# An adapter's up product folded into the next weights, one root for double norms, attention dots in column parts, and a narrow matrix in three parts

## What is computed

```python
# L0 graph attention, second layer (one head): two dots per node, then a softmax over its edges
alpha_s = einsum('nhc,hc->nh', h, a_s); alpha_d = einsum('nhc,hc->nh', h, a_d)
# L2 graph block: adapter, then two graph convolutions (A: the 128 x 128 normalised adjacency)
h = relu(x @ Wd + bd) @ Wu + bu + x        # 768 -> 24 -> 768, with residual
h = relu(A @ (h @ W1) + b1)                # 768 -> 256
h = A @ (h @ W2) + b2                      # 256 -> 768
# L2 ffn: two quantised products of rms-normed rows, 768 -> 2*32 and 32 -> 768
# L3 graph block: relu(A1 @ (xn @ W1) + b1), then A1 @ (. @ W2) + b2, both 768 x 768
# L3 ffn: a router and an attention, each on a layernorm of the block's layernormed rows; MLP 768 -> 48 -> 768
```

## Time and profile before

| | before |
|---|---|
| median of 3 runs | 376.37 us |
| the profiled execution: time, span | 376.2 us, 374.4 us |
| PE busy | 360.3 us, 96% of the span |
| PE in the chain that ended last (VectorE) | 91% (7%) of the span |
| VectorE, ScalarE, GpSimd busy | 180.8, 65.9, 42.1 us |
| granted TensorE clock, mean | 0.986 |
| read from HBM | 89.45 MB, 240 GB/s over the span |

### The profile page before, as it was taken

The page is one execution under the profiler, slowest core; times in us unless marked ns, Lnnn a source line. Parts: engine busy times, 40 slices in busy tenths (PEclk is TensorE's granted clock), DMA queues, the critical chain, the costliest instruction groups (busy, mean ns, idle before and its releaser), DMA issues.

```text
span 374.4 us, 4198 instructions
## 1 busy us (share of the span) xinstructions
PE 360.3 (96%) x1596; PEld 228.4 (61%) x1596; DVE 180.8 (48%) x542; ACT 65.9 (18%) x152; POOL 42.1 (11%) x70
## 2 busy tenths in 40 slices
PE   7999999899999999898899999989999999999997
PEld 3566665556565765555456555464565599966654
DVE  4936525584847465467626635426622301163341
ACT  2012110101111200112002311023123311064010
POOL 4900000020000002040040000302030200000000
PEclk9999999999999999998999999999969999999999
DMA  7999999987955253099999999746251600000001
GB/s 281 412 403 425 437 414 417 370 342 277 348 207 217 105 207 134 15 428 412 412 419 380 420 430 372 289 188 246 63 213 27 268 2 0 2 0 3 0 0 42
DMA packets 10453, 90.10 MB, mean 241 GB/s; under 512 B 2146, under 2 KB 2786, under 8 KB 6338
## 3 DMA queue, kind: packets, MB, share of 16 engines
q1 hardware_dynamic: 8238, 84.91, 56.7%
q0 software_dynamic: 800, 3.54, 2.5%
q10 hardware_dynamic: 1396, 1.40, 1.1%
HBM read 89.45 MB, written 0.39 MB: 240 GB/s over the span
## 4 chain that ended last, share of the span: by engine, by line
PE 91%; DVE 7%; issue 1%; POOL 0%; ACT 0%; POOLq 0%; DVEq 0%
PE ps L1486 14%; PE ps L1452 13%; PE ps L1837 8%; PE ps L1431 6%; PE ps L1664 4%; PE ps L1645 4%; PE ps L1474 3%; PE ps L1751 2%; PE ps L1363 2%; PE ps L1515 2%; PE ps L1817 2%; PE ps L1913 2%; PE ps L1703 2%; PE ps L1885 2%; PE ps L1933 2%; PE ps L1553 2%
## 5 line engine op out<-in xcount | busy, mean ns | idle before, releaser
L1452 PE MATMUL ps<-ring,xT 128*128 128x512 f32 (+1 forms) x168 | 56.4, 486 | 0.0
L1486 PE MATMUL ps<-ring,h 128*128 128x512 f32 (+1 forms) x168 | 55.6, 486 | 0.0
L1486 PEld LDWEIGHTS ps<-ring,h 128*128 128x128 f32 x168 | 31.2, 190 | 21.9 <-issue 20.1
L1452 PEld LDWEIGHTS ps<-ring,xT 128*128 128x128 f32 x168 | 30.8, 191 | 19.5 <-issue 17.7
L792 DVE CUSTOM_DVE_ANT_0 g<-h,avec 128x768 f32<-128x768 f32 x9 | 8.6, 959 | 36.3 <-ACT h L500 24.8
L375 POOL TENSOR_TENSOR rstd<-var,mhalf 128x1 f32<-128x1 f32 x10 | 6.5, 646 | 170.4 <-DVE var L734 83.2
L1431 PE MATMUL ps<-ring,xT 128*128 128x512 f32 (+1 forms) x72 | 24.2, 490 | 0.1
L500 ACT ACTIVATE h<-ps 128x768 f32<-128x768 f32 (+6 forms) x22 | 13.3, 614 | 61.6 <-PE ps L1452 16.2
L880 DVE TENSOR_SCALAR ring<-ring,idxb,ewb 128x128 bf16<-128x128 bf16 x99 | 22.5, 311 | 0.0
L1431 PEld LDWEIGHTS ps<-ring,xT 128*128 128x128 f32 x72 | 13.6, 193 | 9.3 <-issue 8.5
L500 ACT ACTIVATE xT<-ps 128x256 f32<-128x256 f32 (+2 forms) x20 | 7.9, 394 | 56.9 <-PE ps L1379 30.1
(11 more groups left out here) (383 smaller groups left out, 520.4 us busy)
## 6 DMA issues: line engine op xcount, KB each, us to landing
ring<-in_gat_w SPq DMA_DIRECT2D x15, 2304.0 KB, 11.1
avec<-in_gat_a SPq DMA_DIRECT2D x9, 768.0 KB, 8.9
ring<-in_l_w SPq DMA_DIRECT2D x3, 2304.0 KB, 34.3
ring<-in_gat_w SPq DMA_DIRECT2D x6, 384.0 KB, 6.3
ring<-in_l_w SPq DMA_DIRECT2D x2, 1152.0 KB, 6.3
ring<-in_l1f_w1a SPq DMA_DIRECT2D x1, 2304.0 KB, 21.2
ring<-in_l1f_w1b SPq DMA_DIRECT2D x1, 2304.0 KB, 25.8
ring<-in_l1f_w2a SPq DMA_DIRECT2D x1, 2304.0 KB, 30.8
```

The lines of the kernel that those rows point to most:

```text
L1452: last = mm(ps[:, at + lo:at + hi], xT[:, c, :], w[:, c, lo:hi], start=(c == 0), stop=(c == C - 1))
L1486: last = mm(ps[:, 4 * WIN + lo:4 * WIN + hi], h2[:, par * D + c * P:par * D + (c + 1) * P], w[:, c, lo:hi], start=False, stop=False)
```

## The change

- The up product and `l2_w1` are multiplied with each other first (25 x 256), from the weights alone: six small transposes of `l2_wu`, a ScalarE copy, six matmuls, a ScalarE copy to `up_first`. They stand where fillers stood in the first block's ffn end. In the L2 graph block `xT @ l2_w1` starts on the rows themselves, one 25-row matmul adds the adapter, and the adjacency is applied to 256 columns instead of 768.
- The second norm's root is one power of the first variance: 1/sqrt(v(1+e2) + e1 e2). In the L3 ffn both roots come from one two-column instruction, and `xn` is computed later.
- Head 8's dots are taken in two parts: 512 columns from `h1`, 256 columns from PSUM; then a two-element sum. Fifteen edges instead of eight stand behind `score_row`.
- `middle_weights` has three parts of 256 columns; the third stands behind the ffn, between the two halves of L1782, and the L3 stage works in column halves around it. The fold rows of the MLP's norm are made two at a time (2-column outputs) and stand behind the adjacency.
- FIRST_SLOT is 0: units 0 to 3 go into the slots of the head weights as these come free; unit 4 is the first to wait for `edges_summed`.

The core of the diff (index shifts of semaphore counts left out):

```diff
@@ units, names
-FIRST_SLOT = 4
+FIRST_SLOT = 0
-        mhalf = sb("mhalf", [P, 1])
+        mhalf2 = sb("mhalf2", [P, 2])
+        mhalf = mhalf2[:, 0:1]
         released = [("l0_weights_used", 1), ("rows_ps", 6), ("hid1_mm", 2), ("hid1_mm", 4), ("w2a_used", 1),
-                    ("rows_ps", 8), ("rows_ps", 10), ("early_ps", 4), ("rows_ps", 14)]
+                    ("rows_ps", 8), ("rows_ps", 10), ("early_ps", 6), ("rows_ps", 14)]
+        twice, both_var, both_root = cell("twice"), cell("both_var", 2), cell("both_root", 2)
+        wuT, up_first = attnT[:].rearrange("p a b -> p (a b)")[:, 0:C * (DOWN + 1)], att[0:DOWN + 1].rearrange("p a b -> p (a b)")
@@ sync
             load_avec(7)
             load_w2(6, 0)
+            sp.wait_ge(S["hprod"], 7)
+            load_unit(0)
             load_w2(7, 1)
             load_avec(8)
-            sp.wait_ge(s("edges_summed"), 1)
-            for u in range(len(UNITS)):
+            for u in range(1, len(UNITS)):
+                if u == 1:
+                    sp.wait_ge(S["hprod"], 8)
+                if u == 2:
+                    sp.wait_ge(S["w2_used"], 7)
+                if u == 3:
+                    sp.wait_ge(S["hprod"], 9)
                 if u == 4:
-                    sp.wait_ge(S["hprod"], 7)
...
+                    sp.wait_ge(s("edges_summed"), 1)
@@ gpsimd
-            def inverse_root_twice(k, eps):
-                inverse_root(k)
-                pool.wait_ge(s("rstd_ready"), roots[0])
-                link(pool.tensor_tensor(again[:, 0:1], rstd[:], rstd[:], ALU.mult))
-                link(pool.tensor_tensor(again[:, 0:1], again[:, 0:1], mv[:, 1:2], ALU.mult))
-                link(pool.tensor_scalar(again[:, 0:1], again[:, 0:1], eps, None, ALU.add))
-                link(pool.tensor_tensor(again[:, 0:1], again[:, 0:1], mhalf[:], ALU.pow))
-                pool.tensor_tensor(twice, again[:, 0:1], rstd[:], ALU.mult).then_inc(s("rstd_ready"), 1)
...
+            def inverse_root(k, root=rstd[:], of=var[:], half=mhalf):
+                pool.wait_ge(s("var_ready"), k)
+                pool.tensor_tensor(root, of, half, ALU.pow).then_inc(s("rstd_ready"), 1)
...
-            inverse_root_twice(6, RMS_EPS)
+            inverse_root(6, twice)
...
-            inverse_root_twice(9, LN_EPS)
+            inverse_root(10, both_root, both_var, mhalf2[:])
@@ scalar
+            act.wait_ge(s("l2_ps"), 1)
+            copy(wuT, bank(6, C * (DOWN + 1))).then_inc(s("l2_copied"), 1)
+            act.wait_ge(s("l2_ps"), 2)
+            copy(up_first, bank(1, HID2, 0, DOWN + 1)).then_inc(s("l2_copied"), 1)
             part_T(3)
...
             def middle_weights(n):
-                act.wait_ge(s("early_ps"), 2 + n)
-                copy(wo_mid[:, n * D // 2:(n + 1) * D // 2], bank(3 - n, D // 2, 0, BIT)).then_inc(s("early_copied"), 1)
+                act.wait_ge(s("early_ps"), (2, 3, 6)[n])
+                copy(wo_mid[:, n * 256:(n + 1) * 256], bank((3, 2, 7)[n], 256, 0, BIT)).then_inc(s("early_copied"), 1)
...
-            for n, (lo, hi) in enumerate(HALVES):
-                act.wait_ge(s("early_ps"), 5 + n)
-                copy(g1[:, lo:hi], ps[:, 2 * WIN + lo:2 * WIN + hi]).then_inc(s("early_copied"), 1)
+            act.wait_ge(s("early_ps"), 5)
+            copy(g1[:, 0:WIN], bank(2)).then_inc(s("early_copied"), 1)
+            middle_weights(2)
+            act.wait_ge(s("early_ps"), 7)
+            copy(g1[:, WIN:D], bank(3, D - WIN)).then_inc(s("early_copied"), 1)
+            act.wait_ge(s("early_ps"), 9)
+            nc.scalar.activation(xn[:, WIN:D], bank(3, D - WIN), ACT.Relu).then_inc(s("early_copied"), 1)
             act.wait_ge(s("mlp_ps"), 1)
-            copy(fold_row, bank(7, 2 * MLP, 0, 1)).then_inc(s("mlp_copied"), 1)
+            copy(fold_row, bank(7, MLP, 0, 2)).then_inc(s("mlp_copied"), 1)
+            part_T(7)
             act.wait_ge(s("mlp_ps"), 2)
             copy(fold_rows, bank(7, 2 * MLP, 2 * P)).then_inc(s("mlp_copied"), 1)
@@ vector
+            share = cell("alpha_share", 4)
+            dve.wait_ge(s("gat2_rows"), 1)
...
+            for k in range(2):
+                link(nc.vector.tensor_tensor_reduce(g3[:, 0:WIN], h1[:, 0:WIN], avec[:, k * D:k * D + WIN], 1.0, 0.0, ALU.mult,
+                                                    ALU.add, share[:, k:k + 1]))
             dve.wait_ge(S["hprod"], 9)
+            for k in range(2):
+                link(nc.vector.tensor_tensor_reduce(g3[:, WIN:D], bank(5, D - WIN), avec[:, k * D + WIN:(k + 1) * D], 1.0, 0.0,
+                                                    ALU.mult, ALU.add, share[:, 2 + k:3 + k]))
+            nc.vector.tensor_tensor(alpha[:, 0, :], share[:, 0:2], share[:, 2:4], ALU.add).then_inc(S["alpha_ready"], 1)
             nc.vector.tensor_copy(h1[:, WIN:D], bank(5, D - WIN)).then_inc(S["h_rows"], 1)
-            dve.wait_ge(s("gat2_rows"), 1)
-            head_alphas(8, 0)
+            wait(dve, "alpha_ready", 9)
             head_softmax(8, 0)
...
-            for n, (lo, hi) in enumerate(HALVES):
-                dve.wait_ge(s("l2_ps"), n + 2)
-                nc.vector.tensor_tensor(g1[:, lo:hi], ps[:, lo:hi], xn[:, lo:hi], ALU.add).then_inc(s("node_rows"), 1)
-            part_T(6)
             dve.wait_ge(s("l2_ps"), 4)
-            nc.vector.tensor_scalar(g2[:, 0:HID2], bank(7, HID2), 0.0, None, ALU.max).then_inc(s("node_rows"), 1)
+            nc.vector.tensor_copy(g2[:, 0:HID2], bank(0, HID2)).then_inc(s("node_rows"), 1)
+            dve.wait_ge(s("l2_ps"), 5)
+            nc.vector.tensor_scalar(g1[:, 0:HID2], bank(1, HID2), 0.0, None, ALU.max).then_inc(s("node_rows"), 1)
...
-            nc.vector.tensor_scalar(var[:], mv[:, 1:2], LN_EPS, None, ALU.add).then_inc(s("var_ready"), 1)
+            nc.vector.tensor_scalar(var[:], mv[:, 1:2], 1.0 + RMS_EPS, RMS_EPS * LN_EPS, ALU.mult, ALU.add) \
+                .then_inc(s("var_ready"), 1)
...
-            whiten(10)
-            nc.vector.tensor_scalar(xn[:], x[:], mv[:, 0:1], rstd[:], ALU.subtract, ALU.mult).then_inc(S["dve_step"], 1)
...
+            nc.vector.tensor_scalar(both_var[:, 1:2], mv[:, 1:2], 1.0 + LN_EPS, LN_EPS * LN_EPS, ALU.mult, ALU.add) \
+                .then_inc(s("var_ready"), 1)
+            nc.vector.tensor_scalar(both_var[:, 0:1], mv[:, 1:2], LN_EPS, None, ALU.add).then_inc(s("var_ready"), 1)
...
             affine_T("zhatT_ps", g1, "ln1", "xaT_ready")
+            link(nc.vector.tensor_scalar(xn[:], x[:], mv[:, 0:1], both_root[:, 0:1], ALU.subtract, ALU.mult))
@@ tensor
-            sum_edges(range(10, 25))
+            sum_edges(range(10, 18))
             score_row(8, 0)
-            sum_edges(range(25, EC)).then_inc(s("edges_summed"), 1)
+            sum_edges(range(18, EC)).then_inc(s("edges_summed"), 1)
...
-            stay_warm(1, 0)
+            wait_unit(pe, U_L2)
+            w = unit(U_L2, "l2_wu")
+            for c in range(C):
+                last = tr(bank(6, DOWN + 1, c * (DOWN + 1)), w[:, c * P:(c + 1) * P], ident[0:DOWN + 1, 0:DOWN + 1])
+            last.then_inc(s("l2_ps"), 1)
...
             pe.wait_ge(s("adj_ready"), 2)
-            warm_until(7, "var_ready", 3)
-            warm_until(4, "rstd_ready", 3)
+            w = unit(U_L2, "l2_w1", "p (c n) -> p c n", c=C)
+            pe.wait_ge(s("l2_copied"), 1)
+            for c in range(C):
+                last = mm(bank(1, HID2, 0, DOWN + 1), wuT[:, c * (DOWN + 1):(c + 1) * (DOWN + 1)], w[:, c, :], start=(c == 0),
+                          stop=(c == C - 1))
+            last.then_inc(s("l2_ps"), 1)
+            warm_until(1, "rstd_ready", 3)
             stay_warm(2)
...
-                    last_ = mm(bank(3 - n, D // 2, 0, BIT), woT[:, c * BIT:(c + 1) * BIT],
-                               w[:, c, n * D // 2:(n + 1) * D // 2], start=(c == 0), stop=(c == C - 1))
+                    last_ = mm(bank((3, 2, 7)[n], 256, 0, BIT), woT[:, c * BIT:(c + 1) * BIT],
+                               w[:, c, n * 256:(n + 1) * 256], start=(c == 0), stop=(c == C - 1))
...
-            pe.wait_ge(s("l2_copied"), 1)
-            w = unit(U_L2, "l2_wu")
-            for lo, hi in HALVES:
-                mm(ps[:, lo:hi], zT[0:DOWN + 1, :], w[:, lo:hi], start=True, stop=True).then_inc(s("l2_ps"), 1)
-            mm(bank(7, HID2), ones[0:1, :], row("l2_b1")[0:1, :], start=True, stop=False)
-            aggregate(g1, adj2T, "node_rows", {0: 1, 4: 2})
             w = unit(U_L2, "l2_w1", "p (c n) -> p c n", c=C)
             for c in range(C):
-                wait_T(6, c)
-                last = mm(bank(7, HID2), xT[:, c, :], w[:, c, :], start=False, stop=(c == C - 1))
-            last.then_inc(s("l2_ps"), 1)
-            pe.wait_ge(s("node_rows"), 3)
-            for c in range(2):
-                last = mm(bank(2, P, c * P), g2[:, c * P:(c + 1) * P], adj2T[:], start=True, stop=True)
+                mm(bank(0, HID2), xT[:, c, :], w[:, c, :], start=(c == 0), stop=False)
+            pe.wait_ge(s("l2_copied"), 3)
```

(39 more changed lines are left out.)

75 lines of the change are left out of this document (29 added, 46 removed).

## The result

The changed kernel takes 378.46 us in the median of 17 runs (375.55 to 381.17), the kernel before 376.26 us in 17 runs beside it (372.72 to 376.84): a ratio of 1.007, 95% interval 1.0047 to 1.0094. It is slower by 0.7%, a small difference but one clear of the scatter, where 369.3 us was forecast, with a range from 367.9 to 372.6. The ratios quoted in this document leave out runs over 1.5% above the fastest of a kernel; where some runs have much half clock these are just the ones left out, so the medians say more.

A forecast was written before the change was run, and what follows sets the result against it. PE, busy 96% of the span, was taken as the bound. Gains of 1.0 (dots), 0.1 (fold), 4.8 (L2 block) and 1.2 (L3 block) made 7.1 us: 369.1, or 369.3 against the median; range 367.9 to 372.6.

The forecast's parts named there:

- The sum: Whole kernel: gains of 7.1 us taken from the profiled 376.2 us give 369.1, or 369.3 against the median.
- the L2 block: L2 graph block with its shorter middle_weights parts: early starts at 255.2 instead of 259.98, a gain of 4.8 us.
- Weights: Unit loads behind the first block: U_L2 lands at 178.5, 3 us before the small transposes need it at 181.4.
- rival (4): U_L2 late because units 1 to 3 are late: PE stands 17 us before the transposes, 386 us; chance 0.03.
- L3 graph block: New L3 order takes 9.3 us instead of 10.5: gain 1.2, including a 3.4 us refund of half clock.
- Rival (1): Clock falls in the new L3 order or L2 block: 371.0 if half as long, 372.7 if as long; chance 0.22.
- The dots: Head 8's dots at the first block's end: split dots gain 1.0 us, with the fifteen edges as the bound.
- the thirds: middle_weights parts of 256 columns around the L2 block: first gains 1.3 us, second is 1.33 us shorter.
- The fold's products: Six 256-column products of the up fold in the first block's ffn end: 2.61 us, in place of fillers.
- the fold: Fold of the up product, first block's ffn end: gain 0.2 less 0.1 delay from transposes, 0.1 us.
- rival (3): Early loads share the DMA engines with the last W2, which ends 3 us late: 372.3 us; chance 0.04.
- Rival (2): Handovers cost more, or ScalarE delays PE at early and in L3: four places by 0.5 us, 371.3; chance 0.10.

The follow-up runs named there:

- e7: Changed kernel with the load of U_L2 issued ahead of the two w2 units, run a second time: 375.44 us, ratio 0.9894 to the kernel before.
- e3: Changed kernel with the L3 block back in its old order (middle_weights in two parts, old fold rows), U_L2 still late: 374.67 us, ratio 0.998.
- e5: Changed kernel with U_L2 issued ahead of the two w2 units and the L3 block in its old order: 370.66 us, ratio 0.9847.
- e8: As e5, but with the last attention's dots and the edge sums as before the change: 373.10 us, ratio 0.9908.
- e1: Changed kernel with one edit, the load of U_L2 issued ahead of the two w2 units: 377.06 us, ratio 0.9888.
- e14: Same kernel as e1 and e7 (U_L2 early, new L3 order), run again beside a filled-stop version: 375.03 us, ratio 0.9946.
- e9: Changed kernel with U_L2 early and two filler matmuls in PE's 0.45 us L3 stop for ScalarE's copy: 371.88 us, ratio 0.9904.
- e10: Changed kernel with U_L2 early, new L3 order, L3 bias rows by 128-row instead of 1-row matmuls: 372.33 us, ratio 0.9908.
- e12: Same kernel as e11, run again on another chip: 371.12 us, ratio 0.9879.
- e11: As e5 (U_L2 early, old L3 order), with its L3 bias row by 128-row matmuls: 369.84 us, ratio 0.9854.

## Why the prediction was wrong

The sum stood at 369.1 against the profiled run, which then took 379.78: 10.7 us off. By stretches of the two chains: the aggregation stands 3.75 us later than the 187.7 put down (188.79 less 1.1), the L2 block gave 4.41 instead of 4.8, the L3 block took 14.55 instead of 9.8, and from the L3 product to VectorE's `xb` near the end (375.44, before 371.86) there were 93.58 us instead of 91.80. That is 3.75 + 0.4 + 4.75 + 1.8 = 10.7. The sum's own range, stated as 368.3 to 370.8, is 369.0 to 371.0 by the bounds that it names.

**The step "Weights" failed first.** It had `U_L2` at 178.5, 3 us in time. It landed at 182.2, and PE needed it at 180.65 instead of 181.4. Two numbers were short. The rest of unit 3 behind 157.4 was put at 2.3 us, for which no row is given; in fact it could be issued only at 152.81, unit 2 landed at 156.4, and it ended at 162.6, so that 5.2 were left. The engines, idle in the row of 124 to 130, were full with the early units themselves: from 143.4 to 152.8 their share is 1.00, at 417 GB/s. And the 2.8 units were costed at 6.7 us each; they took 19.6 from 162.6 to 182.2, 7.0 each. The name of rival (4) was right (`U_L2` late, PE standing at the small transposes), its price was not: it took all of units 1 to 3 to be late, and the case between, a unit late by a few us, was not worked out. Its price was 4.6 us in this trace: 1.6 for the wait and 3.0 for what the clock did behind it. The aggregation is yet only 3.75 us later than put down, for in e7, with the clock whole, it stands at 186.82, 0.9 us ahead of the forecast. At least a part of this is that the kernel before had 3.4 us at half clock from 167.4 on (the mean of 0.93 in the earlier trace rows), which the prediction did not take into account.

On this the trace and the Trainium skill partly agree. The rows of the changed kernel and of e3 show the clock at half behind a PE that stood 2 to 2.6 us, while PE was busy again. The page "TensorE: Matmul & The Clock Gate" of the Trainium skill, part "The HAM clock gate", has the clock set by how busy PE was lately. By that rule a wait can cost more than its length; rival (4) had no such term. But in e5's profiled run the clock halved at 270.1 behind 4.1 us in which PE was busy all the time, with 37 records of mostly narrow matmuls, as it did at 273.2 in the kernel before; an idle PE is not what these two show. The stretch ahead of it in e5:

```profile
266.00:270.10 4.10, 4.10 (x37) 2.63 (x35) 2.60 (x7) 1.13 (x4) 1.08 (x2) 0.99 0.81 328
270.10:273.50 3.40, 3.40 (x7) 1.72 (x8) 0.69 (x1) 0.62 (x2) 1.81 (x2) 0.50 0.70 280
```

**"L3 graph block" had the wrong sign.** Of its gain of 1.2 us, 3.4 were a refund of the half clock in the earlier trace rows. That was no property of the order before: e3 and e8 (profiled) and six runs of the kernel before went through the same block at full clock. And where it was gone the old order won back 2.75 us, not 3.4 (10.98 to 8.23), for PE then waits for VectorE's first half of the relu (0.70 us on e8's chain), which a slow PE had covered. The terms of the new order were also small: at full clock 11.49 us instead of 9.8. Bias row and adjacency took 3.16 us together instead of 2.68, the second share 0.69 instead of 0.45, the second adjacency 1.53 instead of 1.34, and the fold of the MLP's rows 1.52 instead of 0.76: a matmul with two rows out cost as much as one with one (0.60 us for six, where twelve had taken 1.11), and I had counted the three 48-column matmuls behind it at 0.2 us, where they took 0.92.

**Rival (1), the clock falls in the new L3 order**, did happen, beyond its price. In the profiled run 10.2 us stood at half clock, 3.06 us in the block and 1.65 in the first half of the product behind it (7.00 us instead of 5.35). I took it as an alternative to the forecast with 22 in 100, when, as the runs now show, the kernel before already had half clock somewhere in 93 of 99.

**What held.** The dots gave 0.85 us (forecast 1.0), and the edges were the bound, as put down. The L2 block gave 4.4 us (4.25 in e7). Without the thirds 4.8 - 2.66 = 2.1 us were forecast, and in e8 the stretch takes 257.03 - 187.60 = 69.43 us, 1.8 less than before. The fold's products took 2.70 us (2.61 forecast) in the cover of the fillers; the six small transposes are paid, so that from the first of them (180.65) to the aggregation e7 takes 6.17 us, where the kernel before took 5.97 from its `comb` transpose at 182.82: the fold costs 0.2 us where 0.1 was to be gained. The last W2 was in time; rival (3) had nothing. Rival (2), dearer handovers, explains 0.4 us in the L2 block.

**The books at full clock.** Dots -0.85, fold +0.2, L2 block -4.25, L3 block +3.3 come to -1.6; the runs say 371.4 against 372.8, -1.4. The late unit takes that back (373.2, an estimate from the common slope), and 14.6 us at half clock against 8.2 add 0.35 x 6.4 = 2.2. Together that is 2.6 us, where the medians are 2.2 apart.

## What to carry to other kernels

Where a trace shows a stretch at half clock, ask first for more runs: a loss that comes and goes in the kernel before is not the change's to win back, and the sum is better made at full clock, with the half clock as a term of its own. A weight whose consumer is moved 60 us ahead has to be moved in the queue as well: here the loads landed in the order of their issue, and a wait that delayed PE by 1.6 us cost 4.6. A part moved out of one block into another is costed with its copy and its stop there: here the new order saved 2.6 us in one block and cost 3.3 in the other.

## What the runs showed of the hardware

The large loads on SyncE's queue landed one behind the other, at 397 GB/s from 162.6 to 182.2 us with the DMA engines full. Putting `U_L2` two places forward brought its last part from 182.2 to 168.2 us (e7) and moved the two w2 units back by about 7 us each, for which no engine on the chain waited. The page "DMA: Bandwidth & Descriptors" of the Trainium skill, section "Queues, rings and completion order", says that each DMA engine consumes one queue's descriptors in ring order, but not that loads complete in that order; in these traces the large ones did both.

In one and the same kernel (e1, e7, e14) the time at half clock ran from 0 to 23.5 us from run to run. Across the kernels it stood in ever other places: at 165 and 250 us in the profiled run of e9, at 173, 184 and 249 in e10's, at 183 in e12's, at 270 in e1's and e5's, nowhere before the last microseconds in e7's, e11's and e14's. Why one run has them and the next doesn't stays open.
